# The second layer's attention output kept in 32 bits ahead of its output projection

## What is computed

```python
scores = jnp.einsum('bnqhd,bnkhd->bnhqk', q, k) / np.sqrt(HD)
probs = jax.nn.softmax(scores, axis=-1)
attn = jnp.einsum('bnhqk,bnkhd->bnqhd', probs, v).reshape(B, nW, W, D)
attn = jnp.einsum('bnwd,ed->bnwe', attn, out_w) + out_b
x = _layernorm(x + attn, ln1_g, ln1_b)
ff = jnp.einsum('bnwf,df->bnwd', jax.nn.relu(jnp.einsum('bnwd,fd->bnwf', x, w1) + b1), w2) + b2
x = _layernorm(x + ff, ln2_g, ln2_b)
```

## Time and profile before

| | us |
|---|---|
| median of 3 runs | 2333.63 |
| lowest, highest | 2331.12, 2341.1 |
| the profiled execution | 2340.18 |
| its span, first to last instruction | 2338.4 |
| TensorE busy | 2203.6 (94%) |
| VectorE busy | 1748.5 (75%) |
| ScalarE busy | 1476.5 (63%) |
| GpSimd busy | 1219.1 (52%) |

### The profile page before, as it was taken

The page is one execution under the profiler, slowest core; times in us unless marked ns, Lnnn a source line. Parts: engine busy times, 40 slices in busy tenths (PEclk is TensorE's granted clock), DMA queues, the critical chain, the costliest instruction groups (busy, mean ns, idle before and its releaser), DMA issues.

```text
span 2338.4 us, 59675 instructions
## 1 busy us (share of the span) xinstructions
PE 2203.6 (94%) x21902; PEld 1605.9 (69%) x21902; DVE 1748.5 (75%) x5668; ACT 1476.5 (63%) x2881; POOL 1219.1 (52%) x1323
## 2 busy tenths in 40 slices
PE   4899999999999999999999999999999999999974
PEld 3677766677776677776677777677777677767653
DVE  5677787777787877787777787777787787787753
ACT  2566666766666666666766666666666666666653
POOL 5255444555444555444555454555555555555544
PEclk8999999999999999999999999999999999999997
DMA  1111111111111111111111111111111111111110
GB/s 44 29 36 30 45 38 45 30 40 29 44 37 45 29 41 30 44 37 45 36 36 31 43 36 45 42 31 34 39 36 45 44 28 38 34 36 45 37 28 19
DMA packets 76181, 86.79 MB, mean 37 GB/s; under 512 B 20624, under 2 KB 55440, under 8 KB 76048
## 3 DMA queue, kind: packets, MB, share of 16 engines
q1 hardware_dynamic: 62368, 52.44, 9.4%
q10 hardware_dynamic: 13680, 33.04, 4.2%
HBM read 18.29 MB, written 16.78 MB: 15 GB/s over the span
## 4 chain that ended last, share of the span: by engine, by line
PE 77%; ACT 7%; DVE 6%; issue 4%; SPq 2%; DMA 2%; POOL 2%; ACTq 0%; POOLq 0%; DVEq 0%
PE ps L981 16%; PE ps L875 10%; PE ps L1077 9%; PE ps L877 9%; PE ps L876 9%; PE ps L1045 5%; PE ps L962 4%; PE ps L939 4%; PE ps L1027 4%; PE ps L993 2%; ACT y L498 2%; SPq L328 2%; PE ps L928 1%; PE ps L1097 1%; DMA ptbd<-et 1%
## 5 line engine op out<-in xcount | busy, mean ns | idle before, releaser
L981 PEld LDWEIGHTS ps<-vg,p 128*128 128x128 f32 x4096 | 506.1, 192 | 40.5 <-issue 6.4
L385 POOL TENSOR_TENSOR rstd<-veps,halfpow 128x4 f32<-128x4 f32 x256 | 260.0, 1016 | 508.5 <-DVE veps L755 508.5
L981 PE MATMUL ps<-vg,p 128*128 128x129 f32 x4096 | 523.6, 277 | 0.9 <-ACT p L529 0.9
L529 ACT ACTIVATE p<-ps 128x512 f32<-128x512 f32 x512 | 292.1, 589 | 143.0 <-PE ps L877 113.0
L710 DVE TENSOR_REDUCE cm<-ps 128x1 f32<-128x512 f32 x512 | 334.9, 680 | 16.5 <-PE ps L939 16.3
L419 POOL TENSOR_TENSOR e<-e,srec 128x512 f32<-128x512 f32 x128 | 134.2, 1049 | 246.2 <-DVE srec L798 246.0
L1077 PE MATMUL ps<-w,hid 128*128 128x128 f32 x2048 | 241.7, 276 | 1.8 <-ACT hid L581 1.7
L1077 PEld LDWEIGHTS ps<-w,hid 128*128 128x128 f32 x2048 | 236.2, 192 | 7.6 <-issue 1.8
L581 ACT ACTIVATE hid<-ps,cols 128x512 f32<-128x512 f32 x256 | 165.9, 685 | 97.0 <-PE ps L877 96.9
L939 PE MATMUL ps<-kgh,qgh 128*128 128x512 f16 x512 | 175.8, 384 | 28.6 <-DVE qgl L704 22.3
L962 PE MATMUL ps<-shift,minus 128*128 128x512 bf16 x512 | 194.5, 380 | 2.0
(11 more groups left out here) (184 smaller groups left out, 5504.3 us busy)
## 6 DMA issues: line engine op xcount, KB each, us to landing
ptbd<-et SPq DMA_DIRECT2D x512, 64.0 KB, 2.1
kbd<-kk SPq DMA_DIRECT2D x512, 32.0 KB, 2.0
out_y<-o_sb ACTq DMA_DIRECT2D x64, 256.0 KB, 2.4
x_sb<-in_x ACTq DMA_DIRECT2D x31, 512.0 KB, 4.0
x_sb<-in_x SPq DMA_DIRECT2D x1, 512.0 KB, 3.4
e<-in_w_t SPq DMA_DIRECT2D x1, 256.0 KB, 3.3
w<-in_w_t SPq DMA_DIRECT2D x1, 256.0 KB, 3.2
hid<-in_in_w_t SPq DMA_DIRECT2D x1, 192.0 KB, 2.6
```

What stands on the lines that cost most here:

```text
L385: g.tensor_tensor(rstd[:, k, h, :], veps[:, k, h, :], halfpow[:], ALU.pow).then_inc(s[f"ln_pow{k}"], 1)
L529: sc.activation(p32[:, c % PRING, :], bank("st", c), ACT.Exp, scale=C ** -0.5).then_inc(s["p_made"], 1)
L981: last = mm(ps[:, b, at:at + PVW], p32[:, c % PRING, part], vg32[:, j, :], start=j == 0 and q % 2 == 0, stop=j == MT - 1, skip_group_check ...
```

## The change

The attention output stays in 32 bits: one tile o32 takes the place of oh and ol, and a 32-bit copy wo of the weights takes the place of their halves. ScalarE's copy writes o32, VectorE's step pv1 is gone from its order, its semaphore with it, and TensorE's out issues one 32-bit matmul per block of 128 tokens, waiting on ScalarE's copy. The bank of pv0 is released by that copy. The setup has one VectorE operation fewer.

```diff
--- before.py
+++ after.py
     "dve": """
         ln_in:1-- turn_p0:0-- turn_p1:0-- qg:0- qg:1- max:0- kg:0- max:1- max:2- kg:1- turn_in:1-- max:3- max:4-
-        max:5- k:1-- max:6- pv1:0-- max:7- maxima:0- out:0-- max:8- max:9- q:1-- max:10- score0:1-- turn_mid:0--
-        prob0:1-- score1:1-- turn_p0:1-- prob1:1-- turn_p1:1-- max:11- down:0-- pv1:1-- max:12- out:1-- max:13-
+        max:5- k:1-- max:6- max:7- maxima:0- out:0-- max:8- max:9- q:1-- max:10- score0:1-- turn_mid:0--
+        prob0:1-- score1:1-- turn_p0:1-- prob1:1-- turn_p1:1-- max:11- down:0-- max:12- out:1-- max:13-
...
-    "score0": ("sub_made", 2, True), "score1": ("sub_made", 2, True), "pv0": ("o_lo", 1, True),
+    "score0": ("sub_made", 2, True), "score1": ("sub_made", 2, True), "pv0": ("o_hi", 1, True),
...
+        wo = sb("wo", [P, P])
...
-        oh, ol = sb("oh", [P, 2, HALF], F16), sb("ol", [P, 2, HALF], F16)
+        o32 = sb("o32", [P, 2, HALF])
...
-                sc.activation(oh[:, h, :], bank("pv0", h), ACT.Copy).then_inc(s["o_hi"], 1)
+                sc.activation(o32[:, h, :], bank("pv0", h), ACT.Copy).then_inc(s["o_hi"], 1)
...
-                halves(OUT)
+                link(v_.tensor_copy(wo[:], wraw[:, OUT, :]))
...
-            def pv1(kind, img, h):
-                dve.wait_ge(s["o_hi"], upto(2 * img + h))
-                v_.tensor_tensor(ol[:, h, :], bank("pv0", h), oh[:, h, :], ALU.subtract).then_inc(s["o_lo"], 1)
-
...
-                pe.wait_ge(s["o_lo"], upto(2 * img + h))
+                pe.wait_ge(s["o_hi"], upto(2 * img + h))
                 for j in range(HT):
                     part = slice(P * j, P * (j + 1))
-                    last = three(bank("out", h)[:, part], oh[:, h, part], ol[:, h, part], wh[:, OUT, :], wl[:, OUT, :])
+                    last = mm(bank("out", h)[:, part], o32[:, h, part], wo[:], start=True, stop=True)
                 last.then_inc(s["out_mm"], 1)
```

More of the change, by code:

```diff
@@ L246, in build @@
             q_hi q_lo k_hi k_lo v_made score_mm smax_made sub_made exp_made ssum_made srec_made prob_made
-            et_made pv_win_mm o_hi o_lo out_mm y_bias y1_made r1_scaled r1_made m_hi m_lo
+            et_made pv_win_mm o_hi out_mm y_bias y1_made r1_scaled r1_made m_hi m_lo
             up_mm hid_made down_mm y2_made t2a_made t2b_made t2_made scaled clipped
@@ L851, in _ @@
                       "turn_in": turned_lo("turn_in", "x_hi", "x_lo"), "q": q, "k": k, "score0": score(0),
-                      "score1": score(1), "prob0": prob(0), "prob1": prob(1), "turn_p0": turn_p(0), "turn_p1": turn_p(1), "pv1": pv1, "out": out_proj,
+                      "score1": score(1), "prob0": prob(0), "prob1": prob(1), "turn_p0": turn_p(0), "turn_p1": turn_p(1), "out": out_proj,
                       "turn_mid": turned_lo("turn_mid", "m_hi", "m_lo"), "down": down, "ln_q": ln_q,
@@ L1111 @@
 SETUP_PSUM = SETUP_FIRST + 1 + 4 + 2
-SETUP_STEPS = SETUP_PSUM + 4 + 1 + 1 + 2 + 2 + 2 + 1 + 1 + 1 + 1 + 1 + 1 + 1 + 1 + 2
+SETUP_STEPS = SETUP_PSUM + 3 + 1 + 1 + 2 + 2 + 2 + 1 + 1 + 1 + 1 + 1 + 1 + 1 + 1 + 2
 def kernel(**inputs):
```

## The result

Over 20 executions each, the changed kernel has a median of 2346.07 us (2338.43 to 2347.65) and the kernel before 2337.99 us (2331.12 to 2341.23). The ratio is 1.0033, 95% interval 1.0024 to 1.0042: slower by a third of a per cent, within the half per cent that was called no difference. The executions fall into two loose groups: before has 8 at 2331 to 2336 and 12 at 2338 to 2341, after has 5 at 2338 to 2343 and 15 at 2345.5 to 2348. Group against group, the distance is 8.4 us in the lower and 6.8 in the upper one, so the difference of the medians, 8.1, is good to a microsecond or so and not better.

What follows compares the result with a forecast made beforehand. TensorE's matmul start distances bound the kernel; 31 x (0.45 - 0.215) = +7.3, less 0.46 and 0.33, gives +6.5 us (+8.0 at the feed-forward price); +7 was taken: 2340.6 us against the median 2333.63, range 2332 to 2349.

Steps and rivals of the forecast that it cites:

- The wait's worth: TensorE's out steps start 0.125 and 0.09 us late waiting on VectorE's subtraction; both delays go, -0.215 us per image.
- The price of 0.89 us: TensorE's out step takes 0.89 us in 32 bits against 0.665 in 16: +0.225 us per half, 0.45 per image.
- the entry into 32 bits costs nothing: Read from the P V step, which starts 0.22 us after the 512-column matmul ahead: switching to 32-bit matmuls adds no time.
- VectorE's 44 us at nothing: VectorE loses 64 subtractions of 687 ns, 44 us in all, priced at no gain in kernel time.
- ScalarE's copy at nothing: ScalarE's copy writing 32 bits instead of 16 still takes 0.60 us: no cost, bounds -0.01 to +0.01.
- The tied waits: TensorE's waits on the queries' low half (18.5 us) and ScalarE's norm (16.1 us) move along with TensorE, unchanged.
- The end: Last image's second out step, on the chain that ends last: y comes earlier without subtraction and hop, -0.46 us.
- The setup's -0.33: One 128x128 subtraction on the setup's chain goes, 0.30 us and its hop: -0.33 us.
- (a): Both out-step delays belong to the step and stay: +14.4 to +16 us less 0.8, 2348 us; chance 0.15.
- (c): Weight loads set the 16-bit out step's pace, 1.2 us per step: -27 us, kernel 2307 us; chance 0.02.
- (b): VectorE's freed time pulls the queries' low half forward, up to 21 us gained: 2320 us; chance 0.06.

Runs made afterwards that it cites:

- the run with the wait alone: Kernel before without VectorE's subtraction and the wait on it, the third 16-bit matmul reading the high half again: median 2333.04 us, ratio 0.9978.
- the subtraction without a reader: Changed kernel with the subtraction put back on VectorE, TensorE waiting for ScalarE's copy only: median 2347.35 us, ratio 1.0045 against before.
- The kernel with late memsets: Kernel before with GpSimd clearing the second half's tiles only after VectorE's setup: median 2328.05 us, ratio 0.9957.
- two products: Kernel before with two 16-bit matmuls per block instead of three, the subtraction and its wait gone: median 2312.55 us, ratio 0.9886.

## Why the prediction was right, and where it was off

- Direction and size: +0.3% forecast, +0.33% measured; +7 us forecast, +8.1 measured. The forecast of 2340.6 rests on a median of three runs; twenty put before at 2337.99, and +7 on that is 2345 against 2346.07. The measured time lay in the range because the range had room for that scatter, not because I knew of two groups: 4.4 of the 5.5 us by which 2340.6 was too low are the median of three, and here luck helped.
- The wait's worth, -0.215 us per image: -0.20 by the run with the wait alone. Reading start distances instead of idle time found it.
- The price of 0.89 us: right for half 1 (0.89), mis-sized for half 0 (0.945). The step that failed is "the entry into 32 bits costs nothing". It was read off a row whose forerunner has 512 columns and used for a step whose forerunner has 128. The term is 0.505 us per image instead of 0.45; by it the sum is 31 x 0.295 - 0.8 = +8.3 instead of +6.5, and the medians differ by 8.1. That the two agree to 0.2 us is in part chance, since the groups differ by 6.8 and 8.4.
- VectorE's 44 us at nothing, ScalarE's copy at nothing (597 ns for both): right by the subtraction without a reader and by the page. The 44 us less of VectorE's busy time that the prediction wanted to see were 36.
- The tied waits: 18.2 and 16.4 us against 18.5 and 16.1. Right.
- The end: -0.46 forecast from the copy to y, -0.43 measured. But from the last image's start to the end after lost some 0.7 us more than its out steps account for (172.9 against 172.3 us), and its first five images took 2.4 us less, part of it in waits for row maxima during the setup (4.4 against 5.9 us). Both are single executions. The kernel with late memsets, whose work at the end is that of before, took 170.9 us for the same last stretch, so 0.7 us there is less than what executions differ by. The setup's -0.33 is therefore neither shown nor refuted.
- Rivals (a) and (c) fell to the runs with the wait alone and with two products, (b) to the subtraction without a reader.

## What to carry to other kernels

Where TensorE is busy throughout, price a change by the distance from start to start, and look for a wait in starts that come late, not in booked idle time: 0.21 us per image stood in no wait list. Three 16-bit products (0.665 us) beat one 32-bit product (0.89) for the same tiles, and taking away a subtraction on an engine with time to spare repays only the wait on it. When executions fall into groups, compare their profiles before the first steady image; here one wait in the setup gained 10 to 12 us, more than the change cost.

## What the runs showed of the hardware that was not expected

A 32-bit matmul step of 128 columns has an entry: nothing when its first weight load can start 0.21 us ahead under a matmul of 512 columns, 0.05 us when 0.05 ahead, 0.07 to 0.08 behind a wait. In 16 bits the same steps are 0.66 to 0.67 us with and without the wait. And a VectorE cast of 4 columns took 9.36 and 9.81 us in the profiled executions of before and after, 0.99 with two products and 0.21 with the subtraction without a reader, all beside the same memsets of GpSimd, and 0.18 without them. In all of these with memsets it ended 0.03 us behind the end of one: GpSimd's memsets of 0.95 us came back to back, and a waiting cast got in after one of them in two executions, and in before was passed over at all ten changes.
